# Skills stage of a four-layer kernel: one accumulator pair, three banks of gate and up products, down product two steps behind, and row fetches moved

## The reference, cut to what matters

```
def _gemma_mlp(x, gate_w, up_w, down_w):
    g = jnp.einsum('bsh,hi->bsi', x, gate_w)
    u = jnp.einsum('bsh,hi->bsi', x, up_w)
    return jnp.einsum('bsi,ih->bsh', jax.nn.gelu(g, approximate=True) * u, down_w)
...
def step(acc, params):
    g, u, d, we = params
    return (acc + we[:, None, None] * _gemma_mlp(x, g, u, d), None)
out, _ = jax.lax.scan(step, jnp.zeros_like(x), (skill_gate, skill_up, skill_down, dense_w.T))
out = out + _gemma_mlp(x, shared_gate, shared_up, shared_down)
```

```
wd = expert_down[fi]
wu = expert_up[fi]
hidden = jax.nn.gelu(jnp.einsum('btd,bthkd->bthk', xn, wd), approximate=False)
hidden = hidden * jax.nn.relu(fs)
return jnp.einsum('bthk,bthkd->btd', hidden, wu)
```

## Time and profile before

| | |
|---|---|
| median of 3 runs | 1690.9 us (1688.8 to 1695.48) |
| profiled execution, its own time | 1689.8 us |
| its span in the profile | 1688.1 us |
| mean granted PE clock | 0.94 of full speed |
| PE busy over the span | 1504.5 us (89%) |
| DVE busy | 1080.0 us (64%) |
| ACT busy | 446.1 us (26%) |
| POOL busy | 462.6 us (27%) |
| DMA | 155.92 MB, mean 92 GB/s |

### The profile page before, as it was taken

The page is one execution under the profiler, slowest core; times in us unless marked ns, Lnnn a source line. Parts: engine busy times, 40 slices in busy tenths (PEclk is TensorE's granted clock), DMA queues, the critical chain, the costliest instruction groups (busy, mean ns, idle before and its releaser), DMA issues. The chain is left out here.

```text
span 1688.1 us, 26682 instructions
## 1 busy us (share of the span) xinstructions
PE 1504.5 (89%) x10586; PEld 924.9 (55%) x10586; DVE 1080.0 (64%) x3225; ACT 446.1 (26%) x687; POOL 462.6 (27%) x392
## 2 busy tenths in 40 slices
PE   7989789999999996898888889899998999698882
PEld 3447678888888884443333333344444558344761
DVE  1539898687877662487785667644783498423745
ACT  2332111111111000232333323321112477413232
POOL 0002323231415405066666575400000000000623
PEclk9999899999999997899999899999999999899865
DMA  8900000000000016365557664420142027000235
GB/s 355 228 9 1 2 2 8 2 9 2 9 2 9 3 32 224 141 196 165 172 164 266 192 208 142 131 112 1 37 163 63 14 83 240 0 7 1 70 124 107
DMA packets 86991, 155.92 MB, mean 92 GB/s; under 512 B 42075, under 2 KB 56532, under 8 KB 84308
## 3 DMA queue, kind: packets, MB, share of 16 engines
q1 hardware_dynamic: 64852, 82.91, 14.9%
q0 software_dynamic: 22016, 71.32, 14.2%
HBM read 141.62 MB, written 16.78 MB: 94 GB/s over the span
## 5 line engine op out<-in xcount | busy, mean ns | idle before, releaser
L514 PE MATMUL peer_ps_h<-all_x,layer_down 128*128 128x256 f32 x768 | 180.0, 388 | 0.0
L650 POOL TENSOR_TENSOR peer_bm<-peer_bm,peer_slots 128x512 f32<-128x512 f32 x36 | 109.0, 3028 | 244.7 <-DVE peer_bm L746 244.7
L1420 PE MATMUL skills_acc<-skills_hid,skills_w 128*128 128x512 f32 x256 | 129.7, 632 | 37.0 <-DVE skills_hid L1153 26.7
L514 PEld LDWEIGHTS peer_ps_h<-all_x,layer_down 128*128 128x128 f32 x768 | 144.3, 192 | 21.7 <-issue 1.9
L553 PE MATMUL peer_ps_o<-peer_hg,layer_up 128*128 128x256 f32 x640 | 142.3, 380 | 0.4 <-DVE peer_hg L778 0.4
L553 PEld LDWEIGHTS peer_ps_o<-peer_hg,layer_up 128*128 128x128 f32 x640 | 120.5, 190 | 20.4 <-issue 3.3
L595 ACT ACTIVATE peer_hg<-peer_ps_h 128x512 f32<-128x512 f32 x96 | 57.3, 597 | 274.6 <-PE peer_ps_h L514 274.6
L1473 PE MATMUL skills_ps_g<-all_x,skills_w 128*128 128x512 f32 x256 | 121.7, 598 | 0.0
L1473 PE MATMUL skills_ps_u<-all_x,skills_w 128*128 128x512 f32 x256 | 120.3, 592 | 0.0
L1420 PEld LDWEIGHTS skills_acc<-skills_hid,skills_w 128*128 128x128 f32 x256 | 50.2, 200 | 104.9 <-issue 65.0
L1487 ACT ACTIVATE skills_act_g<-skills_ps_g 128x512 f32<-128x512 f32 x96 | 56.3, 597 | 194.1 <-PE skills_ps_g L1473 170.3
(11 more groups left out here) (426 smaller groups left out, 2610.1 us busy)
## 6 DMA issues: line engine op xcount, KB each, us to landing
four_ring<-in_l_w SPq DMA_DIRECT2D x8, 1024.0 KB, 4.9
quant_w<-in_l_w SPq DMA_DIRECT2D x32, 256.0 KB, 4.6
all_early<-in_l_w SPq DMA_DIRECT2D x26, 256.0 KB, 3.8
four_skill<-in_skills SPq DMA_DIRECT2D x2, 3072.0 KB
skills_w<-in_skills SPq DMA_DIRECT2D x2, 3072.0 KB
layer_down<-in_down SPq DMA_DIRECT2D x1, 4096.0 KB, 25.5
layer_up<-in_up SPq DMA_DIRECT2D x1, 4096.0 KB, 35.2
expert_rows<-in_up SPq DMA_DIRECT2D x1, 4096.0 KB, 41.2
```

Of the source, the lines that this page charges most:

```text
L514: mm = pe.matmul(ps_h[group % 2][:, r, :], down[:, c, j * P:(j + 1) * P], g.x[:, c, bass.ds(i * PB, PB)], start=(c == 0), stop=(c == C - 1))
L650: pool.tensor_tensor(bm[c % RING][:], bm[c % RING][:], slots[half][:, 2, c * PAIRS:(c + 1) * PAIRS].unsqueeze(2).to_broadcast([P, PAIRS, WJ]),
L1420: mm = pe.matmul(acc[q % 2][c][:], w_down[s][:, m, c * P:(c + 1) * P], hid[j % 4][:], start=(s == 0 and m == 0), stop=(s == 2 and m == M2 ...
```

## The change

It has four parts.

1. Fetches: lora issues group 0 at once and group 1 only after all three `hs` activations (`hs_done` = 3); group 2 moves to the start of the skills stage, without a wait.
2. The down product of step j - 2 instead of j - 1 follows the gate and up product of step j; the last two follow the loop.
3. `ps_g`, `ps_u` and `act_g` get a third buffer, used in steps 26 to 62 (`deep`); in the other steps two are used as before. `last_in` names the step that last used a buffer, and PE and ACT wait for that one. The third `act_g` lies in a part of `g.y`, and the third banks serve as `spare` before and after.
4. There is one pair of accumulators. The first down product of blocks 1, 2 and 3 waits for both copies of the block before (`y_done`).

```diff
-            for n in range(NRING):
-                fetch_rows(pool, g, (g.qw, g.held, g.ring2)[n][:, 0:RROWS * 2 * D].rearrange("p (k n) -> p k n", k=RROWS), n)
+            for n in range(NRING - 1):
+                if n > 0:
+                    pool.wait_ge(hs_done, n_blk)
+                fetch_rows(pool, g, (g.qw, g.held)[n][:, 0:RROWS * 2 * D].rearrange("p (k n) -> p k n", k=RROWS), n)
...
-        act_g = [sb(f"act_g{i}", [P, BLK]) for i in range(2)]
+        act_g = [sb(f"act_g{i}", [P, BLK]) for i in range(2)] + [g.y[:, 0, T - BLK:T]]
...
-        ps_g = [ps(f"ps_g{i}", [P, BLK]) for i in range(2)]
-        ps_u = [ps(f"ps_u{i}", [P, BLK]) for i in range(2)]
-        acc = [[ps(f"acc{k}{c}", [P, BLK]) for c in range(C)] for k in range(2)]
-        spare = acc[1]
+        ps_g = [ps(f"ps_g{i}", [P, BLK]) for i in range(3)]
+        ps_u = [ps(f"ps_u{i}", [P, BLK]) for i in range(3)]
+        acc = [ps(f"acc{c}", [P, BLK]) for c in range(C)]
+        spare = [ps_g[2], ps_u[2]]
...
+        deep = range(n_q + 2, TURN3 - 2)
+        bank = [j % 3 if j in deep else j % 2 for j in range(len(plan))]
+        last_in = [max([i for i in range(j) if bank[i] == bank[j]], default=-1) for j in range(len(plan))]
...
-            for n in range(NRING, NCH):
+            for n in range(NRING - 1, NCH):
                 t, k0 = n // (SLOTS // RROWS), n % (SLOTS // RROWS) * RROWS
                 if t >= 2 and k0 == 0:
                     pool.wait_ge(vstep, marks["eid", t])
-                pool.wait_ge(vstep, marks["used", n - NRING])
+                if n >= NRING:
+                    pool.wait_ge(vstep, marks["used", n - NRING])
...
-                if j % n_q == 0:
-                    if q == 1:
-                        pe.wait_ge(sim_read, 2)
-                    if q >= 2:
-                        pe.wait_ge(y_done, (q - 1) * C)
+                if j % n_q == 0 and q > 0:
+                    pe.wait_ge(y_done, q * C)
...
                 if j == TURN3:
                     pe.wait_ge(vstep, marks["used", NCH - 1])
-                    pe.wait_ge(y_done, 2 * C)
+                    pe.wait_ge(hid_done, deep[-1] + 1)
...
+                if j == deep[0]:
+                    pe.wait_ge(sim_read, 2)
-                for weight, bank, free, ready in ((w_gate[s], ps_g[j % 2], gelu_done, g_ready),
-                                                  (w_up[s], ps_u[j % 2], hid_done, u_ready)):
-                    if j >= 2:
-                        pe.wait_ge(free, j - 1)
+                for weight, to, free, ready in ((w_gate[s], ps_g[bank[j]], gelu_done, g_ready),
+                                                (w_up[s], ps_u[bank[j]], hid_done, u_ready)):
+                    if last_in[j] >= 0:
+                        pe.wait_ge(free, last_in[j] + 1)
...
-                if j:
-                    down(j - 1)
+                if j > 1:
+                    down(j - 2)
+            down(len(plan) - 2)
             down(len(plan) - 1)
...
-                if j >= 2:
-                    act.wait_ge(hid_done, j - 1)
-                act.activation(act_g[j % 2][:], ps_g[j % 2][:], ACT.Gelu_apprx_tanh).then_inc(gelu_done, 1)
+                if last_in[j] >= 0:
+                    act.wait_ge(hid_done, last_in[j] + 1)
+                act.activation(act_g[bank[j]][:], ps_g[bank[j]][:], ACT.Gelu_apprx_tanh).then_inc(gelu_done, 1)
```

More of the change, by code:

```diff
@@ L1152, in hidden @@
                 scale = g.pair_w[:, (q // BPB) * 2 + k:(q // BPB) * 2 + k + 1] if k < 2 else 1.0
[L1153 removed]
+                dve.scalar_tensor_tensor(out=hid[j % 4][:], in0=ps_u[bank[j]][:], scalar=scale, in1=act_g[bank[j]][:],
                                          op0=ALU.mult, op1=ALU.mult).then_inc(hid_done, 1)
@@ L1499, in keep @@
                 for c in range(C):
-                    act.activation(g.y[:, c, q * BLK:(q + 1) * BLK], acc[q % 2][c][:], ACT.Copy).then_inc(y_done, 1)
+                    act.activation(g.y[:, c, q * BLK:(q + 1) * BLK], acc[c][:], ACT.Copy).then_inc(y_done, 1)
             act.wait_ge(block3_step, after["xt_ready"])
```

5 lines of the change are left out of this document (2 added, 3 removed).

## The result

| | before | after |
|---|---|---|
| median (lowest to highest) | 1691.4 us (1688.8 to 1695.5, 4 runs) | 1665.9 us (1662.1 to 1669.1, 4 runs) |
| profiled execution, its span | 1688.1 us | 1667.4 us |
| mean granted PE clock | 0.94 | 0.949 |

The ratio is 0.985, with a 95% interval of 0.9827 to 0.9873: 25.5 us less, by the medians. The forecast was 1677.5 us and the range 1662 to 1697. The profiled execution of after was the slowest of its four, so that the two traces differ by 20.7 us, and those are the microseconds that can be followed.

A forecast was written before the change was run, and what follows sets the result against it. The prediction took DVE's chain as the pace from step 3 to TURN3, with stops beside POOL's fetch runs. Terms -15.1 - 1.6 + 1.7 - 0.3 + 2.3 = -13.0 gave 1677.5 us, range 1662 to 1697.

The forecast's parts named there:

- Lora: Moved fetches let ACT's third `hs` start near 661.3 instead of 676.38, -15.1 us; faster PE passes behind it, -1.6.
- the first: Rival: lora's stop stays or moves, 1693.5 us; if group 1 stops the gate chain, some 5 us gain remain; chance 0.2.
- third rival: Group 2's run stops DVE or ACT at the start of skills, nothing won in lora: +14.1, 1704 us; chance 0.08.
- The end of skills: From TURN3 on: one more down product left, +1.7 us, and longer PE idle with slow products after it, +2.3.
- Banks before TURN3: Three banks in steps 26 to 62 let PE run further ahead of DVE, no gain before TURN3.
- My own sign for this: Sign of being wrong: the 408 us stretch shorter by more than 10 us, giving PE's slack a worth.
- The accumulators at 0: `down` 24, 48 and 72 wait for ACT's two copies, hidden behind 3.43 us of PE work: 0 us.
- The cause of the stops: ACT and DVE starve now and then, in lora and skills, while POOL issues fetches without pause; mechanism not named.
- the second rival: PE was the pace after all, so one more step of slack removes gaps: near 1638 us; chance 0.07.
- the -0.3: Start of skills: one down product no longer lies ahead of step 2, where DVE waited 0.31 us for PE.
- the bounds of the terms: Gain of 11.4 to 16.7 us in lora, cost of 1.4 to 3.7 in skills: 1675 to 1683 us.
- The rival with 0.2: By the skill's rule POOL's run is no cause, so lora's stop stays or moves: 1693.5 us, no measurable change; chance 0.2.

The follow-up runs named there:

- e1: The kernel before with the moved fetches alone: 1676.4 us, ratio 0.9901.
- e2: The changed kernel with the three fetch groups issued in lora as before, so the skills edits alone: 1688.8 us, ratio 0.9976.
- e12: The kernel of e7 once more, on a fourth chip where the kernel before took 1695.5 us: 1665.5 us, ratio 0.9828.
- e10: The changed kernel, unchanged, on a third chip: 1624.0 us, ratio 1.0018.
- e8: The changed kernel with the down product one step behind instead of two, on the second chip: 1631.0 us, ratio 1.0059.
- e3: The changed kernel with seven of eight row fetches left out from group 3 on: 1622.4 us, ratio 0.9588.
- e7: The changed kernel, half of each fetch group waiting for earlier row products, ACT's small Gelu behind the odd step's gate Gelu; second chip: 1606.0 us, ratio 0.9902.
- e9: The kernel before, unchanged, on the third chip: 1622.2 us.
- e5: The changed kernel with fetches of 256 bytes a row instead of 2 KB from group 3 on, second chip: 1623.2 us, ratio 1.0007.

## Why the prediction was right or wrong

**Lora: right, in size and place, on this chip.** Forecast -15.1 - 1.6 = -16.7, measured -15.9 by the two traces (ACT's third `hs` 15.3 us earlier) and -18.1 in e1. Group 1's run did not stop the gate chain, and group 2's did not stop the start of skills: neither the first nor the third rival came.

**The end of skills: right.** Forecast +1.7 for one down product and +2.3 for PE's idle time at TURN3, together +4.0; measured +4.7 (181.55 - 176.86), and +3.4 on the third chip. The idle time was 3.49 us in one piece, not 4.65, and still followed by two slow products; that corrects my reading of the earlier trace rows, where a gap of 3.53 was harmless.

**Banks before TURN3: wrong, and this is the step that failed.** I wrote "these let PE run further ahead of DVE, again no gain before TURN3" and that "the shorter PE gaps are worth nothing". Measured: -9.6 us from `hidden` 26 to 64 (e2: -9.5, e1: -0.1). The argument held for a steady chain, in which DVE never waits for PE; and where the chain is steady, on the third chip, it came out to the tenth, 206.21 for 206.24. It left out that the chain of this trace is not steady. I counted the stops as DVE's time, 58 us (with the routing pieces) that lie on its path whatever PE does; the same stops' cost from 26 to 64 fell from 33.2 to 23.7 us with PE's slack. My own sign for this, the stretch to `hidden` 64 shorter by more than 10 us, was missed by little: 407.5 us became 397.8. e12 shows that ACT and DVE are held up at different moments. With two banks a late engine holds up the next at once; with more work in reserve a part of the delays can lie beside each other. That this is how the 9.6 us come about is argued, not shown: no run took two banks alone or a late down product alone on a chip with stops.

**The accumulators at 0: right for the change, by a wrong reason.** "The copies are two activations of 0.69 us, PE has 3.43 us": PE waited 5.6 us for them in e10, since I priced the copies and not their place in ACT's order. The cover is the second step of slack; without it the copies cost 7.0 us in e8.

**The cause of the stops: half right.** That they hang on the fetches was right for chips that have them (e3). That an unbroken run of POOL is enough to make them is wrong: runs of 63 (e10) and 127 fetches (e7) went without any. That POOL's pause ends them fits 13 of 16 in e12, where a pause of 1.03 us was enough for ACT; but a stop also fills the ring and so brings the pause about, and the mechanism stays open. Whether shorter runs would avoid them was not tested, since e12's runs stayed at 16 to 23 fetches. What I had as a property of the kernel is one of the chip, or of the time at which it was used. Held against e9, the kernel before loses 19.2 us in lora (702.93 - 683.70), 18.1 up to `hidden` 26 and 33.2 up to 64: 70.5 together, where the spans differ by 69.9. The change takes back 15.9 of the first piece and 9.6 of the third.

So the second rival, with PE's slack removing gaps, came in part, at 9.6 us of its 40.

**The total.** The sum was -13.0; the traces say -20.7: -9.6 that was not in it, -1.4 at the start of skills beyond the -0.3 forecast, +1.6 in steps 2 to 26, +0.7 at the end, +0.8 in lora, +0.2 behind. The other 5 us up to the 25.5 of the medians are the profiled execution's place among its four. The -0.3 itself came (`hidden` 2 follows 1 after 4.89 us, where it was 5.17). The -1.4 is the first gate product, on PE:

```profile
702.93 3.32 PE L1473 MATMUL skills_ps_g<-all_x,four_skill 128*128 128x512 f32 x4
```

```profile
687.04 1.88 PE L1478 MATMUL skills_ps_g<-all_x,four_skill 128*128 128x512 f32 x4
```

Before, it ran at a granted clock of 0.54 (702.9 to 706.1 us), after at 1.00. It takes 1.88 us in e1 and e2 too, but 3.48 in e10, so it does not come of the edits; what it comes of is open.

The range held the time, and 1677.5 was high by 0.7%. In this there is luck: the bounds of the terms were 1675 to 1683, and the time lies 9 us below them. It is in the range only by the 10 us added for stops that fall otherwise, and the 9.6 us that were missed are of that size by chance. On a chip without stops the sum without its lora terms, +3.7, is what remains; 2.7 us were measured by the medians, of which the part behind `hidden` 64 has +3.4 in the traces and step 15 gives 1.8 back.

**The Trainium skill's two rules.** On chips two and three, "DMA: Bandwidth & Descriptors", section "Queues, rings and completion order", and "Runtime: NRT & Kernel Launch", section "Instruction fetch mechanics", fit what is seen: nothing waits beside POOL's runs. On chips one and four the traces contradict what I drew from them. The rival with 0.2 was built on them, and on two of the four chips the case went as that rival said.

## What to carry to other kernels

Before a stall is priced as part of a kernel, take its trace on a second chip: here 70 of 1690 us, and the whole gain of the change (0.985 or 1.002), differ from chip to chip. If idle time has no releaser that the program knows, a buffer between two engines can be worth something even if the mean pace says that the later one is the bound. Price a copy by its place in its engine's order and not by its duration, and when an edit gives up a buffer, ask which other edit of the same change covers it. Look in the trace whether an edit that should pace an engine does pace it, before its time is read as a test: here the runs stayed whole. The kernel of e7 beats both kernels without stops (0.990); with stops it has 0.983, and the interval of that (0.978 to 0.988) holds the change's 0.985. Its worth without stops lies in one moved line.

## What the runs showed of the hardware that I had not expected

- The same program took 1693.1, 1622.0, 1621.4 and 1695.5 us on four chips, at like clocks (0.94 and 0.956 in the profiled executions of the kernel before), each within about 1% over 7 to 21 runs.
- On two of them ACT, DVE and PE stand still for 2 to some 17 us now and then (ACT for 16.87 us in e2) while POOL's indirect fetches go on, and with an eighth of the fetches they don't (e3). No transfer that the profile calls an instruction's lies in the stretch of the stop that ends at 928.62; the DMA queues of the kernel before from 911 to 935 us (packets, MB, share of 16 engines):

```profile
q0 software_dynamic: 1327, 4.32, 51.0%
q1 hardware_dynamic: 55, 0.96, 9.6%
```

- Where there are stops, most of the long ones end within 0.2 to 3.2 us of the moment at which POOL pauses in its fetches (13 of 16 in e12).
- An indirect fetch of 128 rows costs POOL the same whether a row has 2 KB or 256 bytes: 46 successive ones started within 59.53 us in e10 (869.94 to 929.47) and within 59.52 in e5.
